# Experts and combination of a soft mixture of experts in one block: slot outputs read back by chunks, eight banks, first weights loaded early

## The reference, cut to what matters

```python
def _L1_ffn_ref(x, phi, ln_g, ln_b, w1, b1, w2, b2):
    phi_n = phi * jax.lax.rsqrt(jnp.sum(jnp.square(phi), axis=0, keepdims=True) + EPS_NORM)
    logits = jnp.einsum('bmd,npd->bmnp', x, phi_n)
    D = jax.nn.softmax(logits, axis=1)
    C = jax.nn.softmax(logits.reshape(bsz, m, n * p), axis=-1)
    Xs = jnp.einsum('bmd,bmnp->bnpd', x, D)
    hdn = _layernorm(Xs, ln_g[:, None, :], ln_b[:, None, :])
    hdn = jax.nn.gelu(jnp.einsum('bnpd,ndh->bnph', hdn, w1) + b1[:, None, :], approximate=False)
    Ys = (jnp.einsum('bnph,nhd->bnpd', hdn, w2) + b2[:, None, :]).reshape(bsz, n * p, d)
    return jnp.einsum('bsd,bms->bmd', Ys, C)
```

## Time and profile before

| | us |
|---|---|
| median of 3 runs | 2311.82 (2307.82 to 2313.21) |
| the profiled execution, its own time | 2307.28 |
| its span, first to last instruction | 2305.2 |
| dispatch ends (last copy of ACT) | 2061.76 |
| first expert matmul | 2067.05 |
| last expert matmul ends | 2221.33 |
| first combination matmul | 2231.81 |
| last output tile computed | 2302.39 |

### The profile page before, as it was taken

The page is one execution under the profiler, slowest core; times in us unless marked ns, Lnnn a source line. Parts: engine busy times, 40 slices in busy tenths (PEclk is TensorE's granted clock), DMA queues, the critical chain, the costliest instruction groups (busy, mean ns, idle before and its releaser), DMA issues. The chain is left out here.

```text
span 2305.2 us, 40865 instructions
## 1 busy us (share of the span) xinstructions
PE 2133.9 (93%) x14425; PEld 1913.5 (83%) x14425; DVE 1339.5 (58%) x3473; ACT 1111.3 (48%) x2104; POOL 851.1 (37%) x760
## 2 busy tenths in 40 slices
PE   6999999999999999999999987797599799979988
PEld 5889998999999999999999986797556467769988
DVE  5776667667667667667667654341268466742222
ACT  4556655555555555555555553222244256643310
POOL 4445555555555555555555542110232001000000
PEclk9999999999999999999999998898799899989999
DMA  8400000000000000000000022249200011139966
GB/s 271 144 4 4 4 4 4 8 6 4 8 6 4 8 6 4 6 8 4 4 9 3 1 67 73 78 133 281 72 18 16 0 41 68 54 116 325 326 205 212
DMA packets 101811, 150.30 MB, mean 65 GB/s; under 512 B 14164, under 2 KB 79614, under 8 KB 100988
## 3 DMA queue, kind: packets, MB, share of 16 engines
q1 hardware_dynamic: 78316, 118.36, 16.2%
q10 hardware_dynamic: 17744, 20.27, 2.7%
q0 software_dynamic: 5568, 9.27, 1.4%
HBM read 102.32 MB, written 45.50 MB: 64 GB/s over the span
## 5 line engine op out<-in xcount | busy, mean ns | idle before, releaser
L506 POOL TENSOR_TENSOR t_rstd<-t_var,t_minus_half 128x4 f32<-128x4 f32 (+1 forms) x379 | 367.0, 968 | 629.8 <-DVE t_var L426 628.3
L317 PE MATMUL banks<-t_wt,t_l 128*128 128x256 f32 (+1 forms) x2836 | 596.1, 349 | 0.0
L317 PEld LDWEIGHTS banks<-t_wt,t_l 128*128 128x128 f32 x2836 | 509.8, 192 | 51.0
L380 ACT ACTIVATE t_sq<-banks 128x512 f32<-128x512 f32 (+1 forms) x379 | 215.9, 570 | 567.2 <-PE banks L317 565.8
L434 DVE TENSOR_TENSOR t_yn<-banks,t_rstd 128x512 f32<-128x512 f32 (+1 forms) x379 | 248.9, 657 | 368.1 <-POOL t_rstd L506 368.1
L308 PE MATMUL banks<-t_wt,t_l 128*128 128x128 f32 x2836 | 386.7, 279 | 4.3 <-ACT t_l L398 2.9
L308 PEld LDWEIGHTS banks<-t_wt,t_l 128*128 128x128 f32 x2836 | 356.3, 194 | 14.4 <-ACT t_l L398 3.9
L512 POOL TENSOR_TENSOR t_zrstd<-t_zvar,t_minus_half 128x8 f32<-128x8 f32 x188 | 307.6, 1637 | 12.2 <-DVE t_zvar L470 12.2
L414 ACT ACTIVATE t_l<-banks,t_cols 128x512 f32<-128x512 f32 x376 | 286.3, 776 | 27.9 <-PE banks L370 24.4
L398 ACT ACTIVATE t_l<-banks,t_cols 128x512 f32<-128x512 f32 (+1 forms) x381 | 284.7, 747 | 12.0 <-PE banks L330 6.8
L423 DVE TENSOR_REDUCE t_ss<-t_sq 128x4 f32<-128x512 f32 (+1 forms) x379 | 244.6, 645 | 75.8 <-ACT t_sq L380 68.6
(11 more groups left out here) (335 smaller groups left out, 3425.6 us busy)
## 6 DMA issues: line engine op xcount, KB each, us to landing
t_w<-in_w SPq DMA_DIRECT2D x64, 480.0 KB
t_w<-in_w SPq DMA_DIRECT2D x27, 576.0 KB, 5.5
ect<-t_ECT SPq DMA_DIRECT2D x16, 750.0 KB, 3.2
t_l<-in_w1a SPq DMA_DIRECT2D x27, 384.0 KB, 5.0
sorted_by_expert<-t_h SPq DMA_DIRECT2D x4, 2400.0 KB, 11.6
routed_by_expert<-t_h SPq DMA_DIRECT2D x4, 2400.0 KB, 18.2
t_ectb<-ect ACTq DMA_DIRECT2D x5, 1500.0 KB, 8.0
t_w1x<-in_w1x SPq DMA_DIRECT2D x64, 97.5 KB
```

What stands on the lines that cost most here:

```text
L317: mm = pe.matmul(psY[bank][:, t * C:end * C], src[:, at:at + P], weights[:, C:(1 + end - t) * C], start=False, stop=(t + 1 == n))
L380: act.activation(T["sq"][:, par, 0:n], psY[bank][:, 0:n], ACT.Square).then_inc(S["squared"], 1)
L506: pool.tensor_tensor(T["rstd"][:, par, 0:n], T["var"][:, par, 0:n], T["minus_half"][:, 0:n], ALU.pow)\
```

## The change

- SP loads the weights of experts 0 and 1 at the start of dispatch, into tiles that live beside dispatch's; the experts' block loads 2 to 7 at its start. The ring of 8 is split into two allocations. The memset of `a2` moves to POOL in dispatch, and its block is gone.
- Experts and combination are one block. The experts' waits, orders and rings stay.
- For batches 0 and 1, POOL reads the slots back during the experts: chunk c (128 slots) of each, 96 KB apiece, when the stores of experts up to 8c+7 have landed and chunk c-1 has its bias. DVE adds the bias chunk by chunk, chunk c-2 behind the slot inputs of experts 8c to 8c+7.
- PE, behind the last `down`, sums chunks 0 to 6 of all six tiles of batches 0 and 1 into halves of banks 4 to 6, and then adds chunk 7 to each. The other 18 tiles go round eight banks, and a tile waits for the output seven ahead of it instead of two.
- ACT loads batches 2 to 7 as before, 2 without waiting. DVE's order keeps the bias of batch b+1 ahead of the outputs of batch b.

```diff
         @block.sync
         def _(sp):
+            for r in range(FIRST_LOADS):
+                expert_load(sp, T, S, io, r, r)
...
+            for r in range(FIRST_LOADS):
+                sp.wait_ge(S[f"expert_loaded{r}"], 32)
...
+            pool.memset(T["a2"][:, :, :], 1.0)
...
-def experts(nc, T, S, io):
+MIX_EARLY = 2
+FIRST_LOADS = 2
...
+def expert_load(sp, T, S, io, n, r):
...
+    PER = SOFT_E // SC
+    BEGUN = TPB * MIX_EARLY
+    place_of = [(4 + k // 2, k % 2) for k in range(BEGUN)] + [((7 + k) % 8, 0) for k in range(TILES - BEGUN)]
+    def out_of(k):
+        bank, half = place_of[k]
+        n = min(TOK, LEN - k % TPB * TOK)
+        return ps[bank][0:n, half * D:(half + 1) * D]
...
-            for r in range(AHEAD):
-                load(sp, r, r)
+            for r in range(FIRST_LOADS, AHEAD):
+                expert_load(sp, T, S, io, r, r)
...
+            def slots_back(c):
+                for r in range(RING):
+                    pool.wait_ge(S[f"y_stored{r}"], 16 + 16 * (c + 1) * PER // RING)
+                if c >= 1:
+                    pool.wait_ge(S["slots_back"], MIX_EARLY * c)
+                for b in range(MIX_EARLY):
+                    src = bass.AP(io["ys"].tensor, (b * SLOTS + c * P) * D, [[D, P], [1, D]])
+                    pool.dma_start(T["yb"][:, b, c, :], src).then_inc(S[f"mix_loaded{b}"], 16)
+            n = 0
+            for c in range(SC):
+                while n < MIX_RING * MIX_PIECES and SOFT_E * (n + 1) // (MIX_RING * MIX_PIECES + 1) <= PER * (c + 1):
+                    weights_of_tokens(n)
+                    n += 1
+                slots_back(c)
...
+            for k in range(BEGUN):
+                if k % TPB == 0:
+                    pe.wait_ge(S[f"mix_ahead{k // TPB}"], 16 * MIX_PIECES)
+                    pe.wait_ge(S["slots_back"], MIX_EARLY * (SC - 1))
+                mix(k, range(SC - 1), first=(place_of[k][1] == 0), last=False)
+            for k in range(0, BEGUN, 2):
+                pe.wait_ge(S["slots_back"], MIX_EARLY * (SC - 1) + (k + 1) // TPB + 1)
+                mix(k, (SC - 1,), first=False, last=False)
+                mix(k + 1, (SC - 1,), first=False, last=True).then_inc(S["mixed"], 2)
+            for k in range(BEGUN, TILES):
+                if k % TPB == 0:
+                    pe.wait_ge(S["yb_ready"], k // TPB - MIX_EARLY + 1)
+                    if k // TPB < MIX_RING:
+                        pe.wait_ge(S[f"mix_ahead{k // TPB}"], 16 * MIX_PIECES)
+                if k == BEGUN + 1:
+                    pe.wait_ge(S["expert_read"], SOFT_E + 2)
+                if k >= BEGUN + 5:
+                    pe.wait_ge(S["mix_out"], k - 7)
+                mix(k, range(SC), first=True, last=True).then_inc(S["mixed"], 1)
...
+            for b in range(MIX_EARLY, B):
+                if b >= MIX_RING:
+                    act.wait_ge(S["mixed"], TPB * (b - MIX_RING + 1))
+                    act.dma_start(T["ectb"][:, b % MIX_RING, :, :], io["ect"][b])\
+                        .then_inc(S[f"mix_again{b % MIX_RING}"], 16)
+                src = bass.AP(io["ys"].tensor, b * SLOTS * D, [[D, P], [P * D, SC], [1, D]])
+                act.dma_start(T["yb"][:, b % MIX_RING, :, :], src).then_inc(S[f"mix_again{b % MIX_RING}"], 16)
...
+            def bias_chunk(c):
+                for b in range(MIX_EARLY):
+                    dve.wait_ge(S[f"mix_loaded{b}"], 16 * (c + 1))
+                    y = T["yb"][:, b, c, :]
+                    dve.tensor_tensor(y, y, T["b2s"][:, c, :], ALU.add).then_inc(S["slots_back"], 1)
+            def bias(b):
+                dve.wait_ge(S[f"mix_again{b % MIX_RING}"], 32 * (b // MIX_RING) + (16 if b % MIX_RING >= MIX_EARLY else 0))
+                dve.tensor_tensor(T["yb"][:, b % MIX_RING, :, :], T["yb"][:, b % MIX_RING, :, :], T["b2s"][:, :, :], ALU.add)\
+                    .then_inc(S["yb_ready"], 1)
...
-            with dve.Fori(0, SOFT_E - RING + 1, RING) as i:
...
+            for c in range(SC):
+                slot_inputs(PER * c, PER * (c + 1))
+                if c >= 2:
+                    bias_chunk(c - 2)
+            for c in range(SC - 2, SC):
+                bias_chunk(c)
...
-                if b + 1 < B:
+                if MIX_EARLY <= b + 1 < B:
...
-                    dve.scalar_tensor_tensor(out=T["o"][0:n, k % 4, :], in0=pO[k % 2][0:n, 0:D], scalar=T["rzc"][0:n, k:k + 1],
+                    dve.scalar_tensor_tensor(out=T["o"][0:n, k % 4, :], in0=out_of(k), scalar=T["rzc"][0:n, k:k + 1],
...
-        def _(pe):
-            for b in range(B):
-                pe.wait_ge(S["yb_ready"], b + 1)
-                for t in range(TPB):
-                    k = TPB * b + t
-                    n = min(TOK, LEN - t * TOK)
-                    if k >= 2:
-                        pe.wait_ge(S["mix_out"], k - 1)
...
+            sb("w12_first", [P, FIRST_LOADS, SOFT_H + SHC * D], on=soft)
+            sb("w1x_first", [D2 + 1, FIRST_LOADS, SOFT_H], on=soft)
+            sb("a2", [D2 + 1, RING, P], on=soft)
...
-            sx("a2", [D2 + 1, RING, P])
...
-            with nc.Block() as block:
-                @block.gpsimd
-                def _(pool):
-                    pool.memset(T["a2"][:, :, :], 1.0)
...
-            experts(nc, T, S, io)
             sx("o", [TOK, 4, D])
-            combine(nc, T, S, io)
...
+            experts_and_combine(nc, T, S, io)
```

More of the change, by code:

```diff
@@ L2235, in _, with weights_of_tokens @@
                     sp.wait_ge(S["expert_out"], i + r + 1)
-                    load(sp, i + r + AHEAD, r)
+                    expert_load(sp, T, S, io, i + r + AHEAD, r)
+            for b in range(B):
+                for t in range(TPB):
+                    k = TPB * b + t
+                    n = min(TOK, LEN - t * TOK)
+                    sp.wait_ge(S["mix_out"], k + 1)
+                    sp.dma_start(io["out"][b, t * TOK:t * TOK + n, :], T["o"][0:n, k % 4, :])\
+                        .then_inc(S[f"stored{k % 4}"], 16)
+            for r in range(4):
+                sp.wait_ge(S[f"stored{r}"], 16 * TILES // 4)
         @block.gpsimd
         def _(pool):
-            for n in range(MIX_RING * MIX_PIECES):
+            def weights_of_tokens(n):
                 pool.wait_ge(S["expert_out"], SOFT_E * (n + 1) // (MIX_RING * MIX_PIECES + 1))
@@ L2272, in products, with mix @@
                     down(i + r, r)
+            def mix(k, chunks, first, last):
+                b, t = k // TPB, k % TPB
+                n = min(TOK, LEN - t * TOK)
+                for c in chunks:
+                    mm = pe.matmul(out_of(k), T["ectb"][:, b % MIX_RING, c, t * TOK:t * TOK + n], T["yb"][:, b % MIX_RING, c, :],
+                                   start=(first and c == 0), stop=(last and c == SC - 1))
+                return mm
             up(0, 0, 32)
@@ L2309, in _, with slot_inputs @@
                 act.wait_ge(S[f"y_stored{r}"], 16 * SOFT_E // RING + 16)
+            for b in range(MIX_EARLY, B):
[5 more added lines that the diff above has]
+                act.dma_start(T["yb"][:, b % MIX_RING, :, :], src).then_inc(S[f"mix_again{b % MIX_RING}"], 16)
         @block.vector
         def _(dve):
+            def slot_inputs(first, end):
+                with dve.Fori(first, end - RING + 1, RING) as i:
+                    for r in range(RING):
+                        dve.wait_ge(S["expert_hid"], i + r + 1)
+                        for name, src, g, rows in (("a1", "H1", "egA", P), ("a2", "H2", "egB", D2)):
+                            dve.tensor_scalar(T[name][0:rows, r, :], T[src][:, bass.ds((i + r) * n_rows, n_rows)],
+                                              T[g][:, 0, bass.ds(i + r, 1)], T[g][:, 1, bass.ds(i + r, 1)], ALU.mult, ALU.add)\
+                                .then_inc(S["slots_ready"], 1)
+            def bias_chunk(c):
[7 more added lines that the diff above has]
+                    .then_inc(S["yb_ready"], 1)
             dve.sem_inc(S["expert_hid"], RING)
@@ L2328, in combine @@
-def combine(nc, T, S, io):
-    pO = T["ps"][0:2]
-    with nc.Block() as block:
-        @block.scalar
-        def _(act):
-            for b in range(B):
[L2336 to L2344, removed]
-            for b in range(B):
-                for t in range(TPB):
-                    k = TPB * b + t
-                    n = min(TOK, LEN - t * TOK)
[L2349 to L2363, removed]
-            for b in range(B):
-                if b + 1 < B:
@@ L2585, in program @@
             sb("rzc", [TOK, TILES], on=soft)
+            sb("w12_first", [P, FIRST_LOADS, SOFT_H + SHC * D], on=soft)
+            sb("w1x_first", [D2 + 1, FIRST_LOADS, SOFT_H], on=soft)
+            sb("a2", [D2 + 1, RING, P], on=soft)
+            for name in ("w12", "w1x"):
+                T[name] = [T[name + "_first"][:, r, :] for r in range(FIRST_LOADS)]
             with ExitStack() as disp:
```

36 lines of the change are left out of this document (14 added, 22 removed).

## The result

The changed kernel takes 2293.86 us in the median of 9 runs (2288.67 to 2302.24), the kernel before, on the same chip, 2307.82 (2304.71 to 2313.21). The ratio is 0.9936, with a 95% interval from 0.9920 to 0.9952: 14.8 us gained, between 11.1 and 18.5. I had forecast 8.5 gained and a range that ends at 2294.0. The direction was right; the size was off, and the time lies 0.14 us outside the range. 4 us of that are the median of before, which was 2311.82 in three runs and 2307.82 in nine. On 2307.8 my sum would have given 2299.3, so by the medians 5.4 us of gain remain to be explained (6.3 by the ratio).

What follows compares the result with a forecast made beforehand. PE narrowly bounds the experts, and the service of queued slot loads the combination. Start -3.3, experts +2.0 and combination -7.2 sum to -8.5 us, from the 2311.8 median to 2303; the 8-in-10 range is 2294 to 2312.

Steps and rivals of the forecast that it cites:

- Start: Into the experts: PE's first expert matmul at about 2063.75 in place of 2067.05, 3.3 us gained.
- Experts: Expert stage: 14 slot reads of 96 KB among nearly full DMA engines, at most 4.4 us, taken as 2.0 lost.
- The case of small transfers at 0.95 us each: Reads during the experts: small transfers cost 0.9 us apiece, 13 lost instead of 2, about 2314; chance 0.05.
- The gap: Between experts and combination: PE goes on at full clock, early six tiles end at E + 15.6, 12.9 us gained for the moment.
- E: The prediction's time mark: the end of the last `down` of the experts.
- What is late next: Combination: PE waits before tile 6, load 3 issued at E + 15.0; the combination as a whole gains 7.2, not 12.9.
- four further loads at 9.09: Combination, after batch 3's bias at E + 27.5: four loads of 9.09 us each give E + 63.9.
- the period is their service, not their issue: Combination loads: they queue behind each other, so their service sets 9.09 us per load, where PE wants 7.8 per batch.
- eight banks help nothing while the slots are what is late: Combination: more PSUM banks bring no gain, because PE waits for the loaded slots.
- my 73.4: End of the combination: PE ends at E + 73.4, where before the last output started at E + 80.6.
- The stores on few engines: Output stores in the combination: fewer than five of 16 engines at work; two stores more in load 3's way are 1.8 us.
- the PE-paced rival: Combination: loads run faster, PE sets the end at E + 64.2; 17.7 gained with start and experts, 2294; chance 0.13.

Runs made afterwards that it cites:

- Reads_twice: Changed kernel with each chunk read of the first seven chunks issued a second time, 14 more reads of 96 KB; ratio to the kernel before 0.9958.
- two_banks: Changed kernel with the 18 later tiles in two PSUM banks by turns instead of eight; ratio to the kernel before 0.9958.
- before_split: Kernel before, with each tile's output store cut into 112 rows and the remaining 13 or 12; ratio to the uncut kernel before 0.9971.
- stores_split: Changed kernel with each tile's output store cut into 112 rows and the remaining 13 or 12; ratio to the kernel before 0.9913.
- batch0_ring6: batch0_first with six output tiles and six semaphores for them instead of four; ratio to the kernel before 0.9914.
- best: batch0_first and stores_split together, on the changed kernel; 2289.67 us in the median, ratio to the kernel before 0.9904.
- batch0_first: Changed kernel with batch 0's three tiles finished before tiles 4 and 5 begin, batch 2's bias before the first outputs; ratio to the kernel before 0.9939.

## Why the prediction was right in direction and too small

- *Start*: 3.3 forecast, 3.24 measured, and the first expert product released by DVE, as said. Right.
- *Experts*: 2.0 lost forecast. Mean against mean 1.1 were lost, with the changed code ranging over 4.3 us, while the two profiles of the changed kernel itself would say 1.2 gained. By the clock, the gains of 14.8 and 13.6 us less the 14.7 of the other two stages leave 0.1 gained or 1.1 lost, each to within 4 to 5 us. So neither sign nor size of this term is shown, only that it is small. Reads_twice shows that the way of the cost, through stores, ACT and gelu, exists. Why gelu comes later in one execution than in another stays open. The case of small transfers at 0.95 us each is refuted: at most 0.5 us per read even in the doubled stream.
- *The gap*: chunk 6 in time, chunk 7 by E + 8.9 (bounded by E + 12.1), six tiles done by E + 15.6, clock 1.0. Right.
- *What is late next*: load 3 at E + 15.0 and PE's wait ahead of tile 6 right. The failing step is "four further loads at 9.09", which rested on "the period is their service, not their issue", and with it "eight banks help nothing while the slots are what is late". I had taken 4 us between a load's issue and the landing of the one ahead for a full queue. two_banks shows that the step depends on it: 9.95 us with 1.0 us of lead, 8.07 with 9 in the changed kernel. Eight banks let PE finish a batch while DVE still waits for the next one's slots, and that gives the lead. Nor was 9.09 the service of the loads alone: with the stores cut in two, before_split does 8.08 on two banks and short leads. Of the 4.3 us missed in the last output, 3.4 are the period (36.36 against 32.93) and 1.3 the bias of batch 3, where I had charged 1.8 for two stores; 0.4 goes the other way, the last tiles. With two banks the last output stands at 75.0, 1.6 from my 73.4.
- *The stores on few engines* were read correctly from the trace, and stores_split and before_split confirm that they slow the loads. The Trainium skill's rule ("DMA: Bandwidth & Descriptors", section Why a DMA increments its semaphore by 16: the largest number up to 16 that divides the rows) fits: 112 rows go to all engines, 125 to five. The trace agrees, with 5 small packets for a store of 125 rows and 29 for the two parts. I used it for 1.8 us of one load and did not see that it also sets the period of the later loads, nor how long a store lasts, and so DVE's waits for a place among the outputs: 19.2 us in the changed kernel, 12.1 in stores_split.
- The sum of the three stages is -3.2 + 1.1 - 11.5 = -13.6 us, inside the measured 11.1 to 18.5, but so it is with any expert term from 3.6 lost to 3.8 gained. The remaining 4 us of my miss in absolute time are the three-run median that I started from.
- That the time lands on the 2294 of the PE-paced rival is luck. It asked for the last output at E + 64.2 and 17.7 us gained; the output came at E + 69.1, and the rest is the lower median of before. Only batch0_ring6 and best reach that pace.

## What to carry to other kernels

Before calling a row of queued transfers a service time, look how far ahead of the previous landing each was issued, and what gates that issue: here it was two PSUM banks, through an in-order engine whose output work stood behind a wait for a load. Look too at what else shares the DMA engines: splitting the output stores brought the period down with the banks left alone. When an early start seems to bring nothing, look for the next in-order wait (a ring of four output tiles, here) before giving up: in the last output batch0_first lost 1.3 us, and with two more tiles or with stores on more engines it won 5 to 7. A stage's time from one profile is worth as little as its own variation allows: 4 us between equal experts here, 0.4 between equal combinations.

## What the runs showed of the hardware that I had not expected

Cutting a store of 125 rows of 768 bytes into 112 and 13 rows made everything around it faster, with twice the number of transfers: 5.2 us in the last output of the kernel before. Its trace shows 5 closing packets for such a store and 29 for the two parts. In the kernel before no engine waited for a store, so the gain came through the loads that shared those few engines. And small reads of 96 KB among nearly saturated DMA engines (98% busy) cost the kernel little: 0.3 us each by the clock when fourteen more were added, 0.5 in the slowest execution.
